# Padding an expert's region in front: a longer table, fourteen clearing transfers fewer

## The reference, cut to what matters

```python
def _L1_ffn_ref(x, gate_w, w1, w2, w3):
    xf = x.reshape(-1, orig_shape[-1])
    probs = softmax(einsum('td,ed->te', xf, gate_w))
    weights, idx = top_k(probs, 2)
    weights = weights / sum(weights, axis=-1)
    x1 = silu(einsum('td,efd->tef', xf, w1))
    x3 = einsum('td,efd->tef', xf, w3)
    out_all = einsum('tef,edf->ted', x1 * x3, w2)
    expert_outs = take_along_axis(out_all, idx)
    return einsum('tkd,tk->td', expert_outs, weights)
```

## Time and profile before

| | |
|---|---|
| device time, median of 3 runs | 1725.74 us (1725.56 to 1727.15) |
| span of the profiled execution, first to last instruction | 1724.1 us |
| what the median lies above that span | 1.6 us |
| PE / DVE / ACT / POOL busy | 1679.7 / 1350.6 / 812.6 / 609.5 us |
| transfers | 273.89 MB, of it written to device memory 65.93 MB |
| mean granted TensorE clock | 0.989 of full speed |

### The profile page before, as it was taken

The page is one execution under the profiler, slowest core; times in us unless marked ns, Lnnn a source line. Parts: engine busy times, 40 slices in busy tenths (PEclk is TensorE's granted clock), DMA queues, the critical chain, the costliest instruction groups (busy, mean ns, idle before and its releaser), DMA issues.

```text
span 1724.1 us, 24432 instructions
## 1 busy us (share of the span) xinstructions
PE 1679.7 (97%) x7020; PEld 1188.6 (69%) x7020; DVE 1350.6 (78%) x3866; ACT 812.6 (47%) x1456; POOL 609.5 (35%) x656
## 2 busy tenths in 40 slices
PE   5999999999999999999999999999999999999995
PEld 4667777777777777777777777777777766667773
DVE  5878888888888787979797979787888776565558
ACT  4535453636363545454544445454545343554431
POOL 3311242424242324233333232332323233567770
PEclk8999999999999999999999999999999999999998
DMA  8949474646373747373737373645546445577758
GB/s 211 201 104 256 100 187 105 178 109 181 99 181 101 182 103 194 97 200 86 202 84 192 85 189 90 174 106 135 144 106 167 99 109 154 191 266 266 237 173 312
DMA packets 172339, 273.89 MB, mean 159 GB/s; under 512 B 14312, under 2 KB 57320, under 8 KB 171952
## 3 DMA queue, kind: packets, MB, share of 16 engines
q1 hardware_dynamic: 163632, 254.63, 56.1%
q0 software_dynamic: 8576, 17.70, 3.2%
HBM read 202.15 MB, written 65.93 MB: 155 GB/s over the span
## 4 chain that ended last, share of the span: by engine, by line
PE 94%; DVE 2%; ACT 1%; issue 1%; DMA 1%; POOL 0%; SPq 0%; POOLq 0%; DVEq 0%; ACTq 0%
PE ps_y L709 26%; PE ps_gate L660 8%; PE ps_gate L661 8%; PE ps_gate L662 8%; PE ps_up L662 8%; PE ps_up L660 8%; PE ps_up L661 8%; PE ps_y L735 4%; PE ps_side L675 3%; PE ps_side L758 1%; PE ps_side L852 1%; PE ps_side L835 1%; PE ps_side L794 1%; PE ps_side L819 1%; PE ps_side L660 1%; PE ps_side L661 1%
## 5 line engine op out<-in xcount | busy, mean ns | idle before, releaser
L918 DVE TENSOR_TENSOR silu_h<-ps_up,silu_h 128x512 f32<-128x512 f32 x618 | 424.0, 686 | 295.3 <-ACT silu_h L1325 243.3
L1325 ACT ACTIVATE silu_h<-ps_gate 128x512 f32<-128x512 f32 x618 | 367.6, 598 | 567.4 <-PE ps_gate L662 565.1
L709 PE MATMUL ps_y<-silu_h,w_dn 128*128 128x512 f32 x1056 | 542.7, 595 | 3.0 <-DVE silu_h L912 3.0
L912 DVE TENSOR_TENSOR silu_h<-coef_b,silu_h 128x512 f32<-128x512 f32 x528 | 386.8, 732 | 13.0 <-DMA coef_b<-coef_kept 9.2
L660 PE MATMUL ps_gate<-xnT,w_gu 128*128 128x512 f32 x528 | 342.7, 649 | 0.0
L709 PEld LDWEIGHTS ps_y<-silu_h,w_dn 128*128 128x128 f32 x1056 | 199.7, 189 | 53.7 <-issue 7.7
L660 PE MATMUL ps_up<-xnT,w_gu 128*128 128x512 f32 x528 | 207.9, 394 | 4.6 <-DVE silu_h L918 4.6
L661 PE MATMUL ps_gate<-xnT,w_gu 128*128 128x512 f32 x528 | 209.4, 397 | 0.0
L662 PE MATMUL ps_gate<-xnT,w_gu 128*128 128x512 f32 x528 | 208.9, 396 | 0.0
L662 PE MATMUL ps_up<-xnT,w_gu 128*128 128x512 f32 x528 | 208.0, 394 | 0.0
L661 PE MATMUL ps_up<-xnT,w_gu 128*128 128x512 f32 x528 | 206.8, 392 | 0.0
(11 more groups left out here) (267 smaller groups left out, 2454.8 us busy)
## 6 DMA issues: line engine op xcount, KB each, us to landing
coef_b<-coef_kept SPq DMA_DIRECT2D x254, 512.0 KB, 6.8
slots_x<-empty SPq DMA_DIRECT2D x15, 2080.0 KB, 12.7
w_block<-w_kept SPq DMA_DIRECT2D x45, 512.0 KB, 3.9
xs<-slots_x SPq DMA_DIRECT2D x37, 260.0 KB, 3.8
y_back<-y_kept SPq DMA_DIRECT2D x15, 512.0 KB, 7.0
w_down<-in_ffn_w SPq DMA_DIRECT2D x45, 128.0 KB, 3.7
w_raw<-in_ffn_w SPq DMA_DIRECT2D x33, 128.0 KB, 7.9
xres<-in_x SPq DMA_DIRECT2D x16, 256.0 KB, 3.1
```

The costliest lines, as they stand in the source:

```text
L709: eng.matmul(ps_y[:, :], w_dn[:, j], silu_h[:, g % HBUFS], start=j == 0, stop=last).then_inc(pe_down)
L912: eng.tensor_tensor(silu_h[:, s], coef_b[:, q % COEF_RING, k], silu_h[:, s], ALU.mult).then_inc(dve_h)
L918: eng.tensor_tensor(silu_h[:, s], ps_up[g % 2][:, :], silu_h[:, s], ALU.mult).then_inc(dve_h1)
L1325: eng.activation(silu_h[:, s], ps_gate[g % 2][:, :], ACT.Silu).then_inc(act_silu)
```

## The change

It moves the padding of each expert's region from the end to the front. A region becomes 16 x 512 rows long: the first 512 are cleared, and the tokens follow from row 512 on. The blocks of an expert are cut so that the last ends with the expert's last token; the first then begins inside the cleared rows. Behind an expert's last token nothing is read, so only the 512 rows in front of each region and the spare part need to be cleared: two transfers of 8 x 512 rows each, issued one behind the other in chunk 1, without a wait between them. POOL's sends wait for these two alone. The table on DVE gets the padding of each expert (`pad_e`), its steps between experts, their sum per block (`pad_of`), and subtracts it from the block's first row. Nothing changes in the arithmetic on the rows, nor in the number of blocks.

```diff
-REGION = SPARSE * CHUNK
-SLOTS = EXPERTS1 * REGION + SPARE1 * CHUNK
+REGION = CHUNK + SPARSE * CHUNK
+SLOTS = EXPERTS1 * REGION + EXPERTS1 * CHUNK
...
-            def clear(c):
-                if c == 0:
-                    eng.wait_ge(pool_clear, 2)
-                    eng.dma_start(slots_x[EXPERTS1 * REGION:].rearrange("(p m r) d -> p m (r d)", p=P, m=SPARE1),
-                                  flat(empty).unsqueeze(1).to_broadcast([P, SPARE1, ROWS * ROW1])).then_inc(zero_out, 16)
-                rows = slots_x[0:EXPERTS1 * REGION].rearrange("(e c p r) d -> c p e (r d)", e=EXPERTS1, c=SPARSE, p=P)[c]
-                eng.wait_ge(zero_out, 16 * (c + 1))
-                eng.dma_start(rows, flat(empty).unsqueeze(1).to_broadcast([P, EXPERTS1, ROWS * ROW1])).then_inc(zero_out, 16)
+            def clear():
+                eng.wait_ge(pool_clear, 2)
+                in_front = slots_x[0:EXPERTS1 * REGION].rearrange("(e q) d -> e q d", e=EXPERTS1)[:, 0:CHUNK]
+                spare = slots_x[EXPERTS1 * REGION:].rearrange("(e q) d -> e q d", e=EXPERTS1)
+                for rows in (in_front, spare):
+                    eng.dma_start(rows.rearrange("e (p r) d -> p e (r d)", r=ROWS),
+                                  flat(empty).unsqueeze(1).to_broadcast([P, EXPERTS1, ROWS * ROW1])).then_inc(zero_out, 16)
...
                     if k == COEF_RING and c == 1:
-                        clear(0)
-                    if k == COEF_RING + (2 if c == 1 else 0) and c < SPARSE:
-                        clear(c)
+                        clear()
...
                     keep(eng.tensor_reduce(ends[:, :], upto[:, :, :], axis=AX, op=ALU.add))
                     wait_own()
+                    eng.memset(pad_e[:, EXPERTS1:EXPERTS1 + 1], 0.0)
+                    keep(eng.scalar_tensor_tensor(pad_e[:, 0:EXPERTS1], tiles_e[:, :], float(CHUNK), left[:, :], ALU.mult, ALU.subtract))
+                    wait_own()
+                    keep(eng.tensor_tensor(pad_step, pad_e[:, 1:EXPERTS1 + 1], pad_e[:, 0:EXPERTS1], ALU.subtract))
...
+                    keep(eng.tensor_tensor(past[:, :, :], numbers.unsqueeze(2).to_broadcast(by_block), ends[:, :].unsqueeze(1).to_broadcast(by_block), ALU.is_ge))
+                    wait_own()
+                    keep(eng.tensor_tensor(past[:, :, :], past[:, :, :], pad_step.unsqueeze(1).to_broadcast(by_block), ALU.mult))
+                    wait_own()
+                    keep(eng.tensor_reduce(pad_of, past[:, :, :], axis=AX, op=ALU.add))
+                    wait_own()
+                    keep(eng.tensor_scalar(pad_of, pad_of, pad_e[:, 0:1], None, ALU.add))
...
-                    eng.tensor_scalar(block_row[:, :], begins[:, :], float(CHUNK), None, ALU.mult).then_inc(dve_table)
+                    keep(eng.tensor_scalar(begins[:, :], begins[:, :], float(CHUNK), float(CHUNK), ALU.mult, ALU.add))
+                    wait_own()
+                    eng.tensor_tensor(block_row[:, :], begins[:, :], pad_of, ALU.subtract).then_inc(dve_table)
...
-                        eng.wait_ge(zero_out, 16 * (c + 2))
+                        eng.wait_ge(zero_out, 2 * 16)
```

More of the change, by code:

```diff
@@ L273, in build_program @@
         ends = sb("ends", [EXPERTS1])
+        spread = upto[:, :, :].rearrange("p e f -> p (e f)")
+        pad_e, pad_step, pad_of = spread[:, 0:EXPERTS1 + 1], spread[:, 9:9 + EXPERTS1], spread[:, 17:17 + BLOCKS1]
         past = sb("past", [BLOCKS1, EXPERTS1])
@@ L1635, in shape_constants @@
     neg_ones = -np.ones((P, P), np.float32)
-    region0 = KEY0 - REGION * np.arange(EXPERTS1)
+    region0 = KEY0 - REGION * np.arange(EXPERTS1) - CHUNK
     steps16 = CHUNK * np.arange(16)
```

## The result

The changed kernel takes 1728.69 us (median of 17 runs, 1727.2 to 1729.86), the kernel before beside it 1725.96 us (17 runs, 1725.18 to 1727.15). The ratio is 1.0016, 95% interval 1.0008 to 1.0023: 2.7 us slower. The interval leaves out 1, so the change costs time; by the forecast's bound of 0.2% it is no change, though the interval's upper end lies just beyond that bound. The forecast was 1728.2 us.

A forecast was written before the change was run, and what follows sets the result against it. PE's own instructions were taken to bound the chunks, and DVE the stretch behind the table. 1724.1 + 2.23 (DVE) + 0.3 (clock) + 0 (transfers) = 1726.6 us span, plus 1.6 to the median: 1728.2 us, range 1726.3 to 1730.0.

The forecast's parts named there:

- the forecast's bound of 0.2%: Whole kernel: 0.2%, 3.5 us, is about what a measurement can tell from no change; no change got 0.80.
- What bounds the kernel: Through the chunks PE's own instructions set the pace, busy 1679.7 of 1724.1 us, so removing fourteen covered transfers gives 0.
- The relief rival: Rival: fewer transfers speed PE's matmuls or tile work in the chunks, 1.8 us in all, giving 1726.4; chance 6%.
- The eight instructions, 2.23 us: DVE's table step: the eight added instructions, each priced from the distance between two starts, sum to 2.23 us.
- the dearer sum of 2.55: DVE's table step: about 2.55 us if the three instructions without a wait cost 0.20 each.
- In full to PE: Behind the table DVE is the bound, so PE's up product and everything behind start later by the same 2.23 us.
- The wait "becomes 4.99": PE's wait for DVE's L918 behind the table was to grow from 2.76 to 4.99 us.
- The clock, +0.3: PE's low clock behind the longer wait was to lose 2.0 us in place of 1.7, so +0.3.
- The rival of a second low stretch: Rival: PE's clock stays low 6.1 us behind the longer wait, 1.3 us more than now; 1729.3 to 1729.6; chance 14%.
- Covered after all: Rival: the added table work is hidden because PE's release hangs on something equally late; 1725.7; chance 4%.
- rows late: Rival: the first blocks' rows land late and PE waits; with 1.5 us or more, above 1729.7; chance 3%.
- The sum: Span 1724.1 + 2.23 + 0.3 = 1726.6 us, plus 1.6 from span to median, gives 1728.2 us.

The follow-up runs named there:

- experiment 2: The changed kernel with its sixteen clearing transfers and their old waits put back: 1728.57 us, ratio 1.0016 to the kernel before.
- experiment 1: The kernel before with only the eight added DVE instructions in its table step, results not used: 1728.25 us, ratio 1.0013.
- experiment 3: The changed kernel with the table's three large added instructions done three times in a row: 1731.52 us, ratio 1.0034 to the kernel before.
- experiment 6: The changed kernel with two buffers for `slot_of` and `gw`, on a second chip: 1778.04 us, ratio 1.003 to the kernel before.
- experiment 10: The changed kernel with 64 unused bytes per partition reserved behind `slot_of`, on a third chip: 1781.09 us, ratio 1.0051 to the kernel before.
- experiment 4: The changed kernel with its table cut into six pieces, one in each of tiles 21 to 26: 1728.17 us, ratio 1.0011 to the kernel before.
- Experiment 12: The kernel before with its own table in five pieces and the first blocks' row steps two tiles later, third chip: 1767.68 us, ratio 0.9972.
- experiment 5: The changed kernel with its table in six pieces and the first blocks' row steps two tiles later, second chip: 1765.70 us, ratio 0.9969.
- experiment 9: The changed kernel with its table in six pieces and first row steps two tiles later, repeated on a third chip: 1767.38 us, ratio 0.9975.
- the last versions: The changed kernel with table split and rows later, ratios 0.9969 and 0.9975, and with second buffers behind all other tiles too, 0.9955.

## Why the prediction was right

*What bounds the kernel.* Right. PE was full from 100 to 1400 us and the removed transfers under it gave nothing, in the change and in experiment 2. One premise was too strong: PE's 44.4 idle us are not all that can be won or lost elsewhere, since its busy time itself moves with the clock (1675.5 us after, 1679.7 before, for the same 7020 matmuls). The relief rival wanted 1.8 us, and experiment 2 excludes that much. The Trainium skill, "DMA: Bandwidth & Descriptors", section "Issuing engines are not separate DMA queues", says that all transfers share the sixteen engines. The trace before agrees: the coefficient tiles issued from 1285 to 1310 us, around a clearing transfer, landed in a median of 7.8 us, those from 1305 to 1325, behind it, in 6.1. PE did not stand still for any of them.

*The eight instructions, 2.23 us.* Measured 2.20 in the trace and 2.2 in experiment 1. The single sizes were off by up to 0.1 and cancelled: 0.29 for 0.39 ahead of `past`, 0.15 for 0.10 at `pad_of`. The three without a wait came at 0.02, 0.09 and 0.15 us, so the dearer sum of 2.55 did not come about; that they overlap shows at L1263, which started 0.15 us after L1262, which lasts 0.24. The prediction took 2.55 as the rule of the Trainium skill ("VectorE: DVE Perf Modes", section "The DRAIN you can't avoid"), and left out a clause of that section: a next instruction that is not held starts earlier. The section does say that leaving out the semaphore saves nothing, and there this trace disagrees: 0.02 to 0.15 us without a wait against 0.19 and more with one.

*In full to PE.* Right: +2.34 at PE's resumed product, of which 0.14 had arisen ahead of the table, and one to one again in experiment 3. The wait "becomes 4.99" held in experiment 2 (5.06) but not in the profile after (6.49). The step mixed two things, the moment of release and the moment at which PE arrives. Only the first sets the time.

*The clock, +0.3.* Measured +0.4 in the one trace of the changed kernel, and that was in part luck. The prediction took the cost from the wait nearest in length, as if the length set it. The traces on record say otherwise:

| trace | long wait, us | PE at the lower clock behind it, us | lost, us |
|---|---|---|---|
| before | 2.76 | 3.4 | 1.7 |
| experiment 6 | 4.65 | 6.0 | 3.0 |
| experiment 2 | 5.06 | 5.5 | 2.8 |
| experiment 1 | 6.47 | 3.8 | 1.9 |
| after | 6.49 | 4.25 | 2.1 |
| experiment 10 | 6.50 | 3.3 | 1.7 |
| experiment 3 | 9.45 | 3.5 | 1.8 |

The time at the lower clock does not grow with the wait; part of the low stretch passes while PE still stands, and that part costs nothing. The rival of a second low stretch (6.1 us, 3.0 lost) did not come about in the changed kernel's trace, but experiment 2, with the same release of PE and the same median, comes near to it and experiment 6 reaches it. In experiment 2 the term is +1.1 (2.8 for 1.7), so it is no constant of the change.

*Covered after all, and rows late.* Neither. SP's first load was at 1441.52, as before (1441.48). Rows late was nearer than its 3% suggests: PE's own lateness hid it, and experiment 4 uncovered a wait of 4.95 us as soon as PE came earlier.

*The sum.* 1728.2 forecast, 1728.69 measured. Trace against trace the span grew by 3.2 where 2.5 was forecast. 0.1 lies in the release (0.14 from ahead of the table, less 0.03 on the eight instructions), 0.1 in the clock, 0.4 in the tail, for which the prediction had no term. The close hit of the medians rests on the table's 2.2; the clock's part by itself, 1.7 to 3.0 us lost where 2.0 was assumed, would allow a microsecond more.

The causes are shown for the table by adding it alone (experiment 1) and by its three large instructions three times (3), and for the transfers by putting them back (2). Experiment 12 agrees, at a resolution of about 2 us. What the first 100 us do differently from trace to trace was not studied; it makes up to 2 us in where the last chunk starts (experiment 1).

## What to carry to other kernels

Find the place where the full engine stands and ask what runs through without a pause up to its release: work added there counts in full, while 30 MB of transfers taken from a stretch in which it never stands count nothing. The same small work may cost little or nothing a few tiles on; but look what is late next (here the rows, 17 us behind) and move both. When a kernel becomes slower evenly and no wait explains it, compare the start of one and the same matmul in both traces, and ask whether an edit has moved the buffers.

## What the runs showed of the hardware that I had not expected

**The clock behind a wait.** The short wait of 1.8 to 1.9 us ahead of the table was followed by 3.4 us at the lower clock in four traces (before, experiments 2, 5 and 9) and by none in six (after, experiments 1, 3, 4, 10 and 12). The length of a wait alone did not decide it; what does stays open.

**Addresses.** 64 bytes more in front of the later tiles cost 6.2 us over 1400 us of full matmuls, 0.4%, by a longer spacing of every matmul. Second buffers behind the other tiles cost nothing up to the last chunk (the `gsel` matmul at 1407.28 for 1407.26). Which tile's address it is, and whether another shift would be harmless, was not tried.

**Chips.** The kernel before takes 1726.1 us on one chip and 1771.8 and 1772.4 on two others. Up to 1400 us they run alike: in kernels whose tiles are not moved the `gsel` matmul comes at 1406.6 to 1407.3 on all three, save for the profiled execution of experiment 1 (1408.9). The difference lies in the blocks of layer 1. Windows of experiment 4 on the first chip and of experiment 9 on the third:

```profile
1460.00:1700.00 240.00, 238.75 (x1057) 168.54 (x1056) 139.91 (x320) 109.26 (x187) 152.19 (x172) 1.00 0.69 226
```

```profile
1460.00:1700.00 240.00, 214.35 (x895) 147.62 (x893) 111.30 (x275) 94.87 (x165) 136.16 (x156) 0.94 0.62 195
```

PE is full on the one and stands for 25.7 of 240 us on the other, with 895 matmuls in place of 1057. The cause stays open: the idle time there is put down partly to "remote" and "issue", which name nothing in the kernel. The scatter is wider too, 8 us instead of 2, so the 5 to 8 us of the last versions rest on ratios from such chips, and their gain on the first chip was not measured.
